# A two-layer decoder on one core: loops over batches and expert tiles written out as straight code

## The reference

```python
x = _layernorm(x + _L0_attn_ref(x, ...))    # a0: 16 heads of 16, scores times a decay table
x = _layernorm(x + _L0_xattn_ref(x, ctx, ctx, mask))   # x0: 16 heads over 64 context rows
x = _layernorm(x + _L0_ffn_ref(x, ...))     # ffn: two butterflies, gelu
x = _layernorm(x + _L1_attn_ref(x, ...))    # a1: 16 heads of 64, rotary q and k, causal
x = _layernorm(x + _L1_xattn_ref(x, ctx, ...))         # x1: 8 heads over 512 + 64 keys
x = _layernorm(x + _L1_ffn_ref(x, ...))     # 8 experts, the top 2 of each row
```

## Time and profile before

| | |
|---|---|
| median of 3 runs | 4235.97 us (4231.28 to 4237.2) |
| profiled execution | 4207.76 us, its span 4205.6 us |
| instructions in the span | 82054 |
| PE busy | 3397.4 us (81%) |
| PEld busy | 2498.6 us (59%) |
| DVE busy | 2157.8 us (51%) |
| ACT busy | 1951.0 us (46%) |
| POOL busy | 936.5 us (22%) |
| mean granted TensorE clock | 0.912 of full speed |

### The profile page before, as it was taken

One profiled execution on the slowest core, in us unless ns is written; L12 is line 12 of the kernel. 1 busy time (PEld: TensorE's weight loads), 2 busy tenths in 40 slices (PEclk: granted clock), 3 DMA queues, 4 the chain that ended last, 5 costly groups with the idle time before them and its releaser, 6 DMA issues. The chain is left out here.

```text
span 4205.6 us, 82054 instructions
## 1 busy us (share of the span) xinstructions
PE 3397.4 (81%) x25752; PEld 2498.6 (59%) x25753; DVE 2157.8 (51%) x6691; ACT 1951.0 (46%) x4754; POOL 936.5 (22%) x724
## 2 busy tenths in 40 slices
PE   6888888858699588888988869999996419999990
PEld 3555555557688366666666657777775306666660
DVE  4776777768677355556555534555554301111116
ACT  4777777823322366555665535656663101111110
POOL 0000000034100566667666400000000350000005
PEclk9999999977799799999999989999998559999995
DMA  2000000010200222212222110000001621000004
GB/s 73 12 13 12 12 12 14 7 47 20 93 1 1 84 61 58 52 49 60 57 59 50 41 48 17 21 21 16 16 17 56 208 84 30 30 30 29 29 29 120
DMA packets 120194, 177.79 MB, mean 42 GB/s; under 512 B 23776, under 2 KB 75424, under 8 KB 119328
## 3 DMA queue, kind: packets, MB, share of 16 engines
q1 hardware_dynamic: 113696, 156.61, 12.7%
q0 software_dynamic: 6144, 16.79, 1.3%
HBM read 90.88 MB, written 32.11 MB: 29 GB/s over the span
## 5 line engine op out<-in xcount | busy, mean ns | idle before, releaser
L893 ACT ACTIVATE a_t<-a_t,a_neg 128x512 f32<-128x512 f32 (+3 forms) x1024 | 642.5, 633 | 8.6 <-DVE a_neg L1070 7.2
L720 PE MATMUL a_T<-ident,a_t 128*128 128x128 f32 x3328 | 506.1, 287 | 106.2 <-ACT a_pT L884 56.0
L884 ACT ACTIVATE a_pT<-a_T 128x512 f32<-128x512 f32 (+3 forms) x896 | 416.5, 501 | 321.9 <-PE a_T L720 320.2
L720 PEld LDWEIGHTS a_T<-ident,a_t 128*128 128x128 f32 x3328 | 383.1, 145 | 300.9 <-issue 281.0
L1065 DVE CUSTOM_DVE_ANT_0 a_t<-a_A,a_table 128x384 f32<-128x384 f32 (+3 forms) x512 | 225.5, 487 | 316.4 <-PE a_A L697 311.2
L1065 DVE CUSTOM_DVE_ANT_0 a_t<-a_A,a_decay 128x512 f32<-128x512 f32 x512 | 322.9, 687 | 96.9 <-PE a_A L685 96.9
L2076 PE MATMUL experts_H<-ex_w,experts_xgT 128*128 x576 | 268.3, 609 | 47.8 <-ACT experts_xgT L2103 47.8
L2126 DVE COPY experts_y<-experts_Y 128x256 f32<-128x256 f32 x72 | 30.5, 424 | 514.2 <-PE experts_Y L2064 514.2
L921 POOL TENSOR_TENSOR a_rsin<-a_rawswapped,a_sin 128x512 f32<-128x512 f32 x128 | 166.8, 1303 | 556.8 <-DMA a_rawswapped<-a_raw 534.5
L2064 PE MATMUL experts_Y<-ex_w,experts_hT 128*128 x1152 | 260.5, 379 | 1.0 <-DVE experts_hT L2135 1.0
L2064 PEld LDWEIGHTS experts_Y<-ex_w,experts_hT 128*128 128x128 f32 x1152 | 218.8, 190 | 61.3 <-issue 35.2
(11 more groups left out here) (278 smaller groups left out, 7043.6 us busy)
## 6 DMA issues: line engine op xcount, KB each, us to landing
a_rawswapped<-a_raw SPq DMA_DIRECT2D x512, 64.0 KB, 2.0
a_invrep<-a_inv_dram SPq DMA_DIRECT2D x64, 256.0 KB, 4.0
ex_w<-in_f_w_dram SPq DMA_DIRECT2D x16, 1024.0 KB, 13.5
moe_sent<-route_zeros SPq DMA_DIRECT2D x1, 9216.0 KB, 29.8
experts_xg<-moe_sent SPq DMA_DIRECT2D x72, 128.0 KB, 2.1
moe_results<-experts_y SPq DMA_DIRECT2D x72, 128.0 KB, 1.7
a_xin<-x_all SPq DMA_DIRECT2D x16, 512.0 KB, 3.5
x_xin<-x_all SPq DMA_DIRECT2D x16, 512.0 KB, 3.4
```

The source lines that it names most:

```text
L720: mm = pe.transpose(bank[:, kt, :], t_of(u, j, kt * P, (kt + 1) * P), sh.ident[:])
L884: nc.scalar.activation(to, of, ACT.Copy).then_inc(t_empty, 1)
L893: nc.scalar.activation(t_of(u_e % U, j, 0, n), t_of(u_e % U, j, 0, n), ACT.Exp, bias=neg[:, slot, j:j + 1], scale=SCALE, accum_out=total[: ...
```

## The change

All `Fori` loops over batches and pairs of tiles become Python loops: the body is written out once for each iteration, and `b` or `pair` is a number. There is no branch left in them. All waits have constants and all places in `x_all` are fixed, but for the expert's number, which stays a register.

```diff
@@ attention, batches (cross_attention_heads has the same, line 1188)
-            with eng.Fori(1, B - 1) as b:
+            for b in range(1, B - 1):
                 body(steady, b - 1, b, prev=True, own=True, nxt=True)
@@ attention, gpsimd
-                with pool.Fori(0, B) as b:
+                for b in range(B):
@@ cross_attention_heads, sync
-            with sp.Fori(1, B) as b:
+            for b in range(1, B):
@@ route, tensor
-            with pe.Fori(0, B) as b:
+            for b in range(B):
@@ route, scalar
-            with act.Fori(0, B) as b:
+            for b in range(B):
@@ route, vector
-            with dve.Fori(0, B) as b:
+            for b in range(B):
@@ experts, steps
-            with eng.Fori(1, TILES // 2 - 1) as pair:
+            for pair in range(1, TILES // 2 - 1):
                 for parity in range(2):
                     step(pair, parity, False, True)
@@ combine, sync
-            with sp.Fori(0, B) as b:
+            for b in range(B):
@@ combine, vector
-            with dve.Fori(0, B // 2) as pair:
+            for pair in range(B // 2):
```

## The result

The straight kernel takes 4178.8 us (median of 4, 4174.7 to 4185.0) beside 4236.6 us of the kernel before on the same chip: 0.9867 of it, 95% interval 0.9851 to 0.9882. That is 57.8 us less; the forecast was 25 us less (4211 us), the range ended at 4192 us. The profiled execution was the slowest of the four (span 4183.2 us, granted clock 0.912 in the mean).

A forecast was written before the change was run, and what follows sets the result against it. TensorE, 81% busy, was taken to bound the kernel, with stalls at taken back edges counting only where nothing else covers them. The terms summed to -24.8 us, from 4236.0 to 4211 us, range 4192 to 4226 us.

The forecast's parts named there:

- term 2: In a0 and a1, constants in place of registers cost +2.0 us each, +4 together.
- term 3: In a1, removing the edges costs 9.2 us: longer waits for GpSimd (line 931), then low-clock work.
- term 1: In a0, removing five taken back edges saves 20.8 us, each way across batches falling to 7.3 us.
- The bound "0" of that term: In a1, removing the edges costs nothing if the waits come to lie otherwise.
- Rival C: In a0, clock falls in all six batches take the gain back: +9 us, 4220 us; chance 0.15.
- x0, router: Shorter VectorE waits behind x0's layer norm (-2.4 us) and behind the router's 7 edges (-3 us).
- Experts, combine, x1: Experts -7 us (shorter wait before line 2076), combine -4.8 us, x1 0 because its stalls are covered.
- The combine's term: In the combine, static rows shorten waits before adds to 0.10 us: 1.3 us a pair, 4.8 over the stage.
- Rival D: In the experts, fetching straight code stalls TensorE 3.06 us in each of 34 pairs: +104 us, 4315 us; chance 0.04.
- From profile to timed runs (+28 us): Whole kernel: timed median lies 28 us above the profiled execution, so a 4183 us profile means 4211 us timed.
- Rival A: Every edge stall counts: a0 gains 20.8 us, a1 18.7, x1 14, giving 4169 us; chance 0.05.
- Rival B: a1 neither gains nor loses: 4202 us, down to 4190 if a0 loses some clock falls; chance 0.2.

The follow-up runs named there:

- one_trip: Straight kernel with each batch and each pair of expert tiles in its own one-trip loop, constants kept, branches left in; 0.9888 of the kernel before.
- all_loops: The kernel before, unchanged, profiled and timed once more on another chip; 4212.8 us.

## Why the prediction was wrong, by its own steps

The stages in both forms, mean us (number of profiled executions), against the terms of the sum:

```
            looped        straight      measured   forecast
a0          781.1 (8)     756.6 (7)      -24.5      -18.8
a1          992.6 (7)     986.4 (8)       -6.2      +11.2
x1          713.2 (5)     711.8 (6)       -1.4        0
x0          198.6 (9)     192.6 (6)       -6.0       -2.4
router       61.2          56.0           -5.2       -3
experts     628.9         621.7           -7.2       -7
combine      80.7 (3)      76.3 (2)       -4.4       -4.8
sum                                      -54.9      -24.8
```

The sum of the stages, 54.9 us, lies near the timed gains of 57.8, 61.1 and 57.2 us on three chips. (x1 looped counts the cheap places; combine the chip without late hand-overs.) Of the 30 us that the sum was short, a1 holds 17.4, a0 5.7, x0 3.6, the router 2.2, x1 1.4. By the steps of the prediction: term 2 was wrong by 14.6 us (10.6 less in place of 4 more), term 3 by 7.1, and the first and last batches of a0 and a1, which it put at nothing, gained 4.1; term 1 promised 2.7 too much.

**Term 2 (constants +4) is the step that failed by most.** It came from a0's steps 0 to 9 of one pair of batches, and I charged a1 the same unread. In a1 it had the wrong sign: the six passages from step 4 to 15 take 533.1 us looped and 526.8 us straight, 1.05 us a batch less, and no looped execution is as short as a straight one. It is no edge: in the earlier trace rows's execution batch 6, which ends without one, takes 88.7 us there like batches 3 to 5, and straight batches 87.8 in the mean; `one_trip`, constants with branches, 88.4. Nor is it the clock: passages with the same 6.8 us at the lower clock take 88.9 us looped and 87.9 straight. Which instruction gains it is not settled. In a0 the reading itself was right: batches wholly at 2.4 GHz take 88.4 or 88.5 us from step 0 to 15 looped, 88.5 to 88.9 straight. What it left out is that fewer straight batches hold a fall of the clock (below).

**Term 3 (a1's edges, +9.2) failed in size.** The mechanism was right: the edge's idle time moved into the wait for line 931 (+9.4 us in the groups above), with the low clock behind it, and the straight ways from step 15 to step 4 are 39.8 us long in the mean, as forecast (40.2). The looped side was wrong. I took the five ways of one execution, four of them 37.6 us, as what the loop costs. Over seven profiles a looped way takes 39.4 us in the mean and anything from 37.3 to 41.6. The records of the clock say why: 15 of the 35 looped ways hold 3.4 us at 1.2 GHz and take 37.3 to 38.1 us, the other 20 hold 6 to 10 us and take 39.9 to 41.6. Of the 40 straight ways 39 are of the second sort (38.5 to 41.2 us). The first profile had four of the first sort in five. The edges' gain or loss is +2 us, not +9.2. The bound "0" of that term was the right place.

**a0.** The edges gave 18.1 us (five looped ways take 54.6 us in the mean, not 57.2; straight 36.5): the 7.3 us were exact. The inner steps did not lose 2 but gained 4.3 us. Rival C had it the wrong way round: in the seven straight profiles the stage has 7 to 10 falls of the clock, 40 to 56 us at 1.2 GHz, in the eight looped ones 13 to 19 and 64 to 94 us. A fall makes a batch longer: of the looped batches 1 to 6, 39 of 48 hold 3 or 10 us at 1.2 GHz and take 90 to 92 us in place of 88.4; of the straight ones 19 of 42 hold 10 us and take 91, the others 88.5 to 88.9. That TensorE falls less often because it does not idle 3 us at each edge is argued, not shown: `one_trip` had no such idleness and 12 falls, 70 us.

**x0, router.** Right in place, short in size. I took as the remainder what straight tails or another chain showed (0.34 and 0.10 us); measured it is 0.09 in x0 and nothing in the router. VectorE's own register instruction before line 1916 went too: its wait there for TensorE fell from 6.64 to 6.51 us. In x0 the whole way across a border gained, 11.7 to 10.8 us.

**Experts, combine, x1:** as predicted, within 1.4 us. Line 2076 waits 0.56 us in every tile. The combine's term was added up wrongly: its rows give 1.32 us a pair, 4.5 us in all without the first add, and not 4.8. Rival D is out: the straight experts are shorter tile by tile, and straight x1 is no longer though TensorE's queue fetches 46 packets in it for 16 looped. Its premise was slightly off, since one packet of TensorE's instruction queue does fall into the experts' loop. That fetching the next block in order is mostly hidden, as the Trainium skill says (page "Runtime: NRT & Kernel Launch", section "Instruction fetch mechanics"), agrees with these rows.

**From profile to timed runs (+28 us).** It gave before's median, but it is no property of the kernel: the straight kernel's profiles lay 3 to 7 us above their medians, `all_loops`'s 2 us. Between chips the combine with and without late hand-overs accounts for 18 us of the 18 to 24. That the first profile of before (combine 81 us) came from a chip unlike that of its timed runs is the likely reading of the 28 us; the records don't say it.

**Rival A** (4169 us) came nearest to the time of all, by luck: a1's and x1's edges are covered, as argued against it. Rival B, with a1's edges at nothing and, in its last words, a0 losing some of its falls (4190 us), is nearest in mechanism.

The best version is the changed kernel itself; keeping a1 looped was no faster.

## What to carry to other kernels

Before one execution's four similar waits become a term of a sum, read a second execution, or price the term by its bounds: behind a clock that falls and rises the same way takes 37 or 41 us. What an idle time at an edge costs is read on both sides, before and behind it: it can turn into the next wait, and the stall can shape the clock of what follows.

A loop whose TensorE body is about as long as what its queue keeps at hand is cheap or dear by its place: an edit in front of it, even one that saves time where it is made, can cost 21 us in a stage that nobody touched. Look at the branch's duration and the instruction packets of every later loop, and prefer straight code there: the six straight x1 stages took 710 to 713 us, with three forms of the code ahead of them.

## What the runs showed of the hardware

- A taken jump back held TensorE's queue 3.3 to 5.1 us with bodies of 1936 records and more, and 0.2 or 3.3 to 4.6 us by its place with 1681. A compare-and-branch with its target right behind it: 67 ns. ScalarE's branches took 45 ns, and its next instruction came, in the kernel before, at most 0.2 us behind a taken one.
- The five edges of one loop need not be alike: two or three of five were held at two of the places.
- With gathers issued by GpSimd under way, hand-overs between VectorE's instructions take 0.5 or 1.2 us in place of 0.10 in some batches, 17 to 21 us over the stage with the longer waits beside them, on three of four chips; with plain transfers of the same bytes, issued by ScalarE, they took 0.10 in the one run.
- The same looped stretch of a1, step 15 to step 4 of the next batch, takes 37.3 to 38.1 us with 3.4 us of it at 1.2 GHz and 39.9 to 41.6 us with 6 to 10 us of it.
